# Query projections of two attention stages as three one-pass products of high and low parts, in place of one fp32 product

## The reference

```python
xn = layernorm(x, g_in)                                   # (2, 1024, 256)
q = (xn @ Wq).reshape(b, n, H, DH).transpose(0, 2, 1, 3) * scale   # Wq: 256 x 1024
kv = xn @ Wkv                                             # 256 x 128
k, v = (kv[..., :DH], kv[..., DH:])
...
sim = jnp.einsum('bhid,bjd->bhij', q, k) + bias           # masked, causal
attn = jax.nn.softmax(sim, axis=-1)
out = jnp.einsum('bhij,bjd->bhid', attn, v)
```

## Time and profile before

| what | value |
|---|---|
| median of 3 executions | 3154.18 us (3151.99 to 3158.55) |
| profiled execution, its own time | 3162.94 us |
| its span, first to last instruction | 3161.2 us |
| mean granted TensorE clock, share of full speed | 0.948 |
| busy TensorE / VectorE / ScalarE / GpSimd | 91% / 58% / 50% / 14% |
| first query stage | 669.7 to 742 us |
| second query stage | 2184 to 2257 us |

### The profile page before, as it was taken

The page is one execution under the profiler, slowest core; times in us unless marked ns, Lnnn a source line. Parts: engine busy times, 40 slices in busy tenths (PEclk is TensorE's granted clock), DMA queues, the critical chain, the costliest instruction groups (busy, mean ns, idle before and its releaser), DMA issues. The chain is left out here.

```text
span 3161.2 us, 50878 instructions
## 1 busy us (share of the span) xinstructions
PE 2875.9 (91%) x17739; PEld 2105.7 (67%) x17741; DVE 1825.0 (58%) x4505; ACT 1575.4 (50%) x3841; POOL 455.9 (14%) x807
## 2 busy tenths in 40 slices
PE   7988999899999999858799999987999999969996
PEld 4746666565777777435577777764577777759995
DVE  5556555256677775786677777445577777440002
ACT  4502555435666662554566666333466666313331
POOL 4460000001111110000000000000011111015553
PEclk8988999899999999878899999998999999969998
DMA  4453221056434431003622221003644444325554
GB/s 124 122 164 68 56 56 29 3 173 206 142 115 147 143 108 41 1 21 100 185 64 88 69 87 52 19 2 132 212 141 143 132 142 128 126 94 180 184 181 134
DMA packets 251734, 340.83 MB, mean 108 GB/s; under 512 B 28573, under 2 KB 186397, under 8 KB 251344
## 3 DMA queue, kind: packets, MB, share of 16 engines
q1 hardware_dynamic: 233098, 277.13, 28.9%
q0 software_dynamic: 18384, 60.44, 6.2%
HBM read 263.83 MB, written 73.21 MB: 107 GB/s over the span
## 5 line engine op out<-in xcount | busy, mean ns | idle before, releaser
L2394 ACT ACTIVATE cond_p<-cond_p,cond_negm 128x128 f32<-128x128 f32 (+7 forms) x768 | 593.1, 775 | 402.3 <-DVE cond_negm L2425 401.7
L2375 PE MATMUL ps_o<-cond_pt,cond_v 128*64 128x256 f32 (+1 forms) x3840 | 479.0, 371 | 5.0 <-DVE attn_out L2461 0.5
L2355 PE MATMUL ps_s<-cond_k_high,cond_q_high 128*128 128x512 f32 (+5 forms) x1152 | 440.0, 388 | 17.8 <-PEq L1844 10.4
L2425 DVE CUSTOM_DVE_ANT_0 cond_p<-ps_s,cond_side,cond_null_scores 128x128 f32<-128x128 f32 (+7 forms) x512 | 403.5, 811 | 29.7 <-PE ps_s L2356 23.4
L2356 PE MATMUL ps_s<-cond_k_both,cond_q_both 128*128 128x512 f32 (+5 forms) x1152 | 394.8, 344 | 0.0
L2375 PEld LDWEIGHTS ps_o<-cond_pt,cond_v 128*64 128x64 f32 x3840 | 237.6, 136 | 180.7 <-issue 90.2
L2365 PE MATMUL ps_t<-ident,cond_p 128*128 128x128 f32 x2304 | 349.1, 281 | 6.9 <-ACT cond_pt L2399 4.8
L2365 PEld LDWEIGHTS ps_t<-ident,cond_p 128*128 128x128 f32 x2304 | 250.2, 141 | 106.5 <-issue 78.0
L1524 ACT ACTIVATE attn_pt<-ps_t 128x512 f32<-128x512 f32 (+3 forms) x384 | 173.3, 490 | 247.3 <-PE ps_t L1485 176.8
L2355 PEld LDWEIGHTS ps_s<-cond_k_high,cond_q_high 128*128 128x128 f32 x1152 | 220.4, 191 | 41.9 <-issue 18.3
L2333 POOL COPY cond_rb<-cond_rinv 128x256 f32<-128x256 f32 x192 | 77.1, 402 | 1156.9 <-DVE cond_rinv L2451 1156.9
(11 more groups left out here) (494 smaller groups left out, 4823.8 us busy)
## 6 DMA issues: line engine op xcount, KB each, us to landing
mqa_q_halves<-cond_q_cut SPq DMA_DIRECT2D x96, 512.0 KB, 4.8
cond_q_both<-mqa_q_halves SPq DMA_DIRECT2D x384, 128.0 KB, 3.1
cond_q_high<-mqa_q_halves SPq DMA_DIRECT2D x192, 128.0 KB, 3.0
cond_side<-in_fside_16xSxS SPq DMA_DIRECT2D x32, 512.0 KB, 7.1
cond_side<-in_fside_16xSxS SPq DMA_DIRECT2D x32, 448.0 KB, 5.6
cond_side<-in_fside_16xSxS SPq DMA_DIRECT2D x32, 384.0 KB, 5.2
cond_side<-in_fside_16xSxS SPq DMA_DIRECT2D x32, 320.0 KB, 4.7
attn_q<-attn_q_halves SPq DMA_DIRECT2D x64, 128.0 KB
```

The source lines that it names most:

```text
L2355: nc.tensor.matmul(out, c32(a.Q1[i][:, h, s * P:(s + 1) * P]), c32(a.K1[:, keys]), start=True, stop=False)
L2375: last = nc.tensor.matmul(sums[u % ON][h * HD:(h + 1) * HD, s0 * P:2 * P], a.V[:, b * QB + kb, :], PT[c % PT_SLOTS][:, (2 * h + s0) * P:(h ...
L2394: nc.scalar.activation(p, p, ACT.Exp, bias=negm[u % SMALL][:, r:r + 1], scale=-1.0, accum_out=rsum[u % SMALL][:, r:r + 1]).then_inc(exped, 1)
L2425: nc.vector.tensor_tensor_reduce(out=probs(u, r, 0, q + 1), in0=m.S[k % 2][:, row_offset(L):row_offset(L) + L], in1=toep_back(u, h, L) if ...
```

## The change

Both query stages of the plain kind get high and low parts of the features (`XH`, `XL`) and of the query weights (`WH`, `WL`, which takes the place of the weights themselves). ScalarE makes the high parts with fp32r copies, VectorE makes the low parts with subtractions. A job is then, for each half of the 256 features, the three one-pass products high x high, high x low, low x high, six fp32r matmuls in all; the product low x low is left out. The keys, the values and the null scores stay fp32. VectorE's fill of the mask row and the ones moves from ahead of the jobs to behind job 20 (`fill_rows`).

```diff
@@ -1699,6 +1699,10 @@
     keyed, k_taken, valued, v_taken, cut_k = (m.sem(f"{name}_{s}") for s in ("keyed", "k_taken", "valued", "v_taken", "k_cut"))
     nulled, weighed, k_cleared = (m.sem(f"{name}_{s}") for s in ("nulled", "value_null_weighed", "k_cleared"))
     q_made, q_high, q_low = (m.sem(f"{name}_{s}") for s in ("q_made", "q_high", "q_low"))
+    x_high, x_low, w_high, w_low = (m.sem(f"{name}_{s}") for s in ("x_high", "x_low", "w_high", "w_low"))
+    XH = m.sb(name + "_x_high", [P, DC, B * S], F32, m.R + 32768)
+    XL = m.sb(name + "_x_low", [P, DC, B * S], F32, m.R + 49152)
+    WH, WL = q.WH, q.WL
     JOBS = PAIRS * NG
     VALUES_AT = 2
     with nc.Block() as block:
@@ -1726,9 +1730,16 @@
                     pe.wait_ge(k_taken, j + 1)
                 else:
                     pe.wait_ge(q_low, j - 3)
+                if j == 0:
+                    pe.wait_ge(w_high, 1)
+                    pe.wait_ge(w_low, 1)
+                if j < NG:
+                    pe.wait_ge(x_low, DC * (g + 1))
+                cols, toks = slice(pair * P, (pair + 1) * P), slice(g * GRP, (g + 1) * GRP)
                 for c in range(DC):
-                    last = nc.tensor.matmul(m.SH[j % 4], wq_all[:, c, pair * P:(pair + 1) * P], m.XT[:, c, g * GRP:(g + 1) * GRP],
-                                            start=(c == 0), stop=(c == DC - 1))
+                    for n, (w_part, x_part) in enumerate(((WH, XH), (WH, XL), (WL, XH))):
+                        last = nc.tensor.matmul(m.SH[j % 4], r32(w_part[:, c, cols]), r32(x_part[:, c, toks]),
+                                                start=(c == 0 and n == 0), stop=(c == DC - 1 and n == 2))
                 last.then_inc(q_made, 1)
 
             pe.wait_ge(loaded, q.n_loads)
@@ -1755,6 +1766,13 @@
 
         @block.scalar
         def _(act):
+            act.wait_ge(loaded, q.n_loads)
+            for g in range(NG):
+                for c in range(DC):
+                    toks = slice(g * GRP, (g + 1) * GRP)
+                    nc.scalar.copy(r32(XH[:, c, toks]), m.XT[:, c, toks]).then_inc(x_high, 1)
+                if g == 0:
+                    nc.scalar.copy(r32(WH[:, :, :]), wq_all[:, :, :]).then_inc(w_high, 1)
             for g in range(NG):
                 act.wait_ge(keyed, g + 1)
                 nc.scalar.mul(KW[:, g * GRP:(g + 1) * GRP], m.SH[g][0:HD, :],
@@ -1777,17 +1795,23 @@
             dve.wait_ge(nulled, 1)
             nc.vector.tensor_tensor(wn[:, :, :], wq_all[:, :, :].rearrange("p c (h w) -> p (c h) w", w=HD),
                                     nk[:, :].unsqueeze(1).broadcast_to([P, DC * HEADS, HD]), ALU.mult).then_inc(nulled, 1)
+            dve.wait_ge(nulled, 2)
+            dve.wait_ge(w_high, 1)
+            low(nc, WL[:, :, :], wq_all[:, :, :], WH[:, :, :]).then_inc(w_low, 1)
+
+            def cut_features(g):
+                for c in range(DC):
+                    toks = slice(g * GRP, (g + 1) * GRP)
+                    dve.wait_ge(x_high, DC * g + c + 1)
+                    low(nc, XL[:, c, toks], m.XT[:, c, toks], XH[:, c, toks]).then_inc(x_low, 1)
+
+            cut_features(0)
+            cut_features(1)
             nc.vector.tensor_copy(VN[:, :, 0:HD], wkv[:, :, HD:2 * HD]).then_inc(weighed, 1)
-            dve.wait_ge(nulled, 2)
             nc.vector.tensor_reduce(VN[:, :, HD:HD + HEADS], wn[:, :, :].rearrange("p (c h) w -> p c h w", c=DC),
                                     mybir.AxisListType.X, ALU.add).then_inc(weighed, 1)
-            dve.wait_ge(k_cleared, 1)
-            nc.vector.tensor_scalar(r32(K1[HD:HD + 1, :]), mask[HD:HD + 1, :], 2.0 ** 100, -2.0 ** 100, ALU.mult, ALU.add)
-            for i in range(Q_SLOTS):
-                nc.vector.tensor_copy(r32(Q1[i][HD:P, :, :]).rearrange("p h (s q) -> p (h s) q", q=P),
-                                      m.ones[HD:P, :].unsqueeze(1).broadcast_to([HD, 4, P]))
-            nc.vector.tensor_copy(nv_wide[:, :], nv[:, 0:1].broadcast_to([P, P]))
-
+            for g in range(2, NG):
+                cut_features(g)
             def take_values_and_nulls(t):
                 dve.wait_ge(valued, t + 1)
                 nc.vector.tensor_tensor(V[:, t, :], m.O[t % 2][:, 0:HD], nv_row[:, :], ALU.subtract)
@@ -1797,6 +1821,14 @@
             def cut_low(j, whole):
                 dve.wait_ge(q_high, j + 1)
                 low(nc, cut[j % Q_CUTS][:, 1, :], whole, cut[j % Q_CUTS][:, 0, :]).then_inc(q_low, 1)
+
+            def fill_rows():
+                dve.wait_ge(k_cleared, 1)
+                nc.vector.tensor_scalar(r32(K1[HD:HD + 1, :]), mask[HD:HD + 1, :], 2.0 ** 100, -2.0 ** 100, ALU.mult, ALU.add)
+                for i in range(Q_SLOTS):
+                    nc.vector.tensor_copy(r32(Q1[i][HD:P, :, :]).rearrange("p h (s q) -> p (h s) q", q=P),
+                                          m.ones[HD:P, :].unsqueeze(1).broadcast_to([HD, 4, P]))
+                nc.vector.tensor_copy(nv_wide[:, :], nv[:, 0:1].broadcast_to([P, P]))
 
             def cut_keys(after):
                 dve.wait_ge(*after)
@@ -1810,6 +1842,8 @@
                 cut_low(j, m.SH[j % 4])
                 if VALUES_AT <= j < VALUES_AT + NT:
                     take_values_and_nulls(j - VALUES_AT)
+                if j == 20:
+                    fill_rows()
                 if j == 24:
                     cut_keys((k_taken, NG))
 
@@ -2076,6 +2110,8 @@
     g_in = m.sb(name + "_g_in", [P, D], F32, loop_at)
     wkv = m.sb(name + "_wkv", [P, DC, 2 * HD], F32, loop_at + 1024)
     mask = m.sb(name + "_mask", [P, B * S], U8, loop_at + 2048)
+    WH = m.sb(name + "_wq_high", [P, DC, HEADS * HD], F32, loop_at + 27648)
+    WL = m.sb(name + "_wq_low", [P, DC, HEADS * HD], F32, loop_at + 8192)
     VN = m.sb(name + "_w_value_null", [P, DC, HD + HEADS], F32, loop_at + 26624)
 
     n_cuts = 4 if cosine else Q_CUTS
@@ -2168,6 +2204,8 @@
     q.cut = cut
     q.wkv = wkv
     q.wq_all = wq_all
+    q.WH = WH
+    q.WL = WL
     q.wn = wn
     q.nv = nv
     q.nv_row = nv_row
```

## The result

| what | before | with the change |
|---|---|---|
| median, executions | 3153.20 us (3145.15 to 3159.41), 12 | 3140.13 us (3131.38 to 3147.58), 12 |
| ratio, 95% interval | 1 | 0.9950 (0.9938 to 0.9962) |
| profiled execution, its own time | 3162.94 us | 3132.53 us |
| its span | 3161.2 us | 3130.8 us |
| granted clock | 0.948 | 0.952 |

The medians differ by 13.1 us; the forecast was 13.8. The two profiled spans differ by 30.4 us, which is not the change's doing alone. The jobs account for 7.36 + 7.88 = 15.24 us. The rest lies almost wholly in stretches with the same code on both sides (7.8 us before the first stage, 3.1 between the stages, 4.4 behind the second) and moves from one execution to the next.

A forecast was written before the change was run, and what follows sets the result against it. TensorE was taken to bound both query stages; shorter jobs, less waits, gain 6.6 and 7.2 us, together 13.8, taking the median from 3154.18 to 3140.4 us, range 3132 to 3149.

The forecast's parts named there:

- The product: TensorE's jobs in both query stages: one fp32r matmul takes 0.233 us, so a job alone falls from 1.72 to 1.40.
- The rival of 216 ns: Each of the six products in a job runs at 216 ns, giving 3134 us; chance 0.12.
- The values: Jobs with value matmuls: 0.44 us for values plus 0.08 for the format change, a job every 1.92 us.
- The entry: Start of each stage: TensorE waits for group 2's low features, 1.3 us in the first stage, 0.7 in the second.
- The keys: VectorE's 4.8 us cut of the keys makes TensorE wait 1.2 us at job 29.
- The fill: VectorE's work moved from the entry to behind job 20: 2.9 us, fitting in the slack there.
- The end: End of each stage: all engines meet, the loop behind is unchanged, so the gain goes through to the end.
- The stores: Query stores of 512 KB take at most 1.43 us each; over the last 14 jobs the DMA loses 0.03 us a job.
- the ring: Store slots, each needed again after 11.2 us; cut, issue, landing and backlog make 9.4, so covered by under 2 us.
- The clock: New waits at job 2 or 29 lower TensorE's clock, 3.4 us a spell; two of four give 3147; chance 0.13.
- The open weight loads: TensorE's 0.19 us weight loads are not hidden beside the product in front: 3212 us, or 3170 if partly; chance 0.04.
- No effect: Products go at fp32 pace or the gain is made up elsewhere, so nothing remains: 3154 us; chance 0.03.

The follow-up runs named there:

- the fourth product: Changed kernel plus the product low x low, eight one-pass products per job: 3150.05 us in one execution, jobs 68.19 us in both stages.
- the repeat: The changed kernel executed again with no edit: median 3133.37 us of 6 executions, ratio 0.9953 to the kernel before.
- the kernel with both edits: Changed kernel with null-score weights summed after job 1, values from job 4, keys cut behind jobs 6, 10, 14: median 3125.05 us, ratio 0.9922 to before.

## Why the prediction was right

**The time.** 3140.4 us forecast, 3140.13 measured. The mechanism held: TensorE set the pace of the jobs before and after, and the shorter products shortened them. The agreement to 0.3 us is luck, since terms of 1 to 3 us were missed both ways; the terms, by the jobs' stretch:

- **The product.** Forecast 0.233 us; measured 0.232 among the values and 0.227 behind them, and the fourth product costs 0.224 to 0.227. A job alone is 1.36 to 1.37 us, not 1.40. The rival of 216 ns fell: none of 384 products came near it over a run of rows.
- **The values.** Forecast 0.44 + 0.08 us. A job with values starts every 1.83 us, not 1.92. The values take 0.36 us; the first product behind them takes 0.31 to 0.32 us, as the earlier trace rows said. The mis-sized term is the 0.44, a difference between two kinds of fp32 jobs, to which I added a change of format; together they came out 0.08 us too long, 1.2 us over 15 jobs.
- **The entry.** Forecast waits of 1.3 and 0.7 us; the rows have 1.06 and 0.37, at the place and with the releaser named. The four subtractions took 2.49 us as costed.
- **The keys.** Forecast 1.2 us; 1.26 and 1.47, at job 29, as said. One reading behind it was wrong: the 1.1 us of the earlier trace rows and the row at 735.12 are waits of the weight loads (PEld), not of the matmuls, which ran without a gap (24.34 us of rows). The cut of the keys cost TensorE nothing before the change.
- **The fill.** Behind job 20 it takes 2.8 us of VectorE and makes nobody wait. That it was moved there is worth more than the forecast thought, as its return to the entry shows.
- **The end.** Not in the sum: 0.8 us a stage for SyncE's slow issues. Up to ScalarE's last copy the jobs gained 8.15 and 8.64 us, 3.0 more than the 13.8 of the forecast, mostly from the shorter jobs; 1.55 of it was given back here. This term was put at nothing, with the sentence that all engines meet at the end and the loop is unchanged.
- **The stores.** This is the step that failed, though its price in the profiled execution was only the 0.2 us behind the keys. I gave the ring under 2 us of cover, from a landing of 5.0 us and a backlog of 3. Landing took up to 8.9 us in the first stage and 10.6 in the second, and ScalarE waited, which the prediction had named as a sign against it. In the other execution of the same kernel that cost 2.1 us. A store takes 1.365 us at 384 GB/s, not the 1.43 of the upper bound, so over the last 14 jobs the DMA fell behind no further than it was; at 1.43 it would have lost 0.07 us on each of them, 1 us in all.

**The rivals.** The clock: no spell in either stage of the profiled execution, but one in the repeat, so the mechanism is real, with one spell in four stages; the chance of 0.13 was given to two or more in the program, which neither trace has. The open weight loads: out. No effect: out.

The difference of the medians itself moved from 13.1 us here to 14.4 on the chip of the repeat, about as much as a term was missed by, so the total could not have told the terms apart.

## What to carry to other kernels

When the engine that sets the pace becomes faster, work out the pace of the next two: here a job fell from 1.72 to 1.36 us, a store takes 1.365, and VectorE's pieces only just fit, so a further third off TensorE's work gained under 1 us. At such a point the order of the small work decides: what delays the first store, or sits in one piece in front of a producer, costs more than its length, because its wait may bring the clock down. Measure a stage from rows that begin behind its own noise; without a wait for the stores the stretch of the jobs repeated to 0.01 us, where the whole program scattered by 14.

## What was not expected of the hardware

- **Waits and the clock.** TensorE at full clock fell to 1.2 GHz behind single waits of 1.93, 2.11, 2.23, 2.34, 2.35, 2.55, 3.05, 3.17, 3.44 and 3.57 us in these runs, and did not behind waits of 1.06 to 1.74 us, of which there were over twenty. Two short ones (1.77 and 1.62 us), 2 and 9 us after another spell, had one behind them; one of 1.60 us, 4 us after a spell, had none. A spell was mostly some 3.5 us with products of 0.427 us, and cost about 1.6 us; the longest took 12 products, 5 us, and cost some 2.4.
- **SyncE's issues grow.** The same store takes 0.36 us to issue at the median with four products (DMA share 0.86) and 0.74 in the first stage of the changed kernel (1.05 in its last 21 us); single issues took up to 1.94 us, and 1.24 in the kernel before. What decides whether the last one is slow is open: the end gap was 2.10 to 2.15 us in 16 of the 26 stages and 2.62 to 3.05 in the other 10, and the kernel with both edits, with its DMA as full (1.05 from 706 to 720 us), had 2.14.
- **GpSimd beside VectorE.** Sharing eight subtractions, the two took 8.5 us from the first start to the last end, where VectorE alone needs 5.0.
- **The product's pace.** 0.232 us among fp32 matmuls and 0.227 without them; why is open. Job 0, with no values yet, had 0.232 as well, and so had job 29 behind the keys' wait, so fp32 neighbours are not the whole of it.
